# Second mixer of a two-layer network: 32x32 image products, norms applied on ScalarE, rows written out, VectorE's chains woven

## The reference, cut to what matters

```
u           = layernorm(x, 1e-6) @ W_in           # z (192), conv part (224 = 192 + 16 B + 16 C), dt (12)
xBC         = silu(conv3x3(conv part) + b_conv)
dt          = softplus(dt + dt_bias);  A = -exp(A_log)
L           = exp(segsum(dt * A))
Y_diag      = einsum('bclhn,bcshn,bhcls,bcshp->bclhp', C, B, L, X)
states      = einsum('bclhn,bhcl,bclhp->bchpn', B, decay_states, X)
Y_off       = einsum('bclhn,bchpn,bhcl->bclhp', C, states, exp(A_cumsum))
y           = layernorm(Y + D_param * X, 1e-5) * gamma + beta
x           = x + (y * silu(z)) @ W_out
```

## Time and profile before

| what | value |
| --- | --- |
| three runs, us | 2660.29, 2666.05, 2674.77 |
| profiled execution, own time | 2666.47 us |
| its span, first to last instruction | 2664.7 us |
| PE busy | 1986.0 us, 75% |
| DVE busy | 1728.5 us, 65% |
| POOL busy | 1371.1 us, 51% |
| ACT busy | 1063.6 us, 40% |
| mean granted TensorE clock | 0.805 |

### The profile page before, as it was taken

The page is one execution under the profiler, slowest core; times in us unless marked ns, Lnnn a source line. Parts: engine busy times, 40 slices in busy tenths (PEclk is TensorE's granted clock), DMA queues, the critical chain, the costliest instruction groups (busy, mean ns, idle before and its releaser), DMA issues.

```text
span 2664.7 us, 63187 instructions
## 1 busy us (share of the span) xinstructions
PE 1986.0 (75%) x24050; PEld 1660.2 (62%) x24050; DVE 1728.5 (65%) x5157; ACT 1063.6 (40%) x1936; POOL 1371.1 (51%) x1285
## 2 busy tenths in 40 slices
PE   3666433249999938999899989999975331699997
PEld 2555433237777727888788778888864331477775
DVE  4778644325766647888888878888856432366665
ACT  2233111037777723433333434333311110477775
POOL 2111155546877725555545545555533555477776
PEclk8667555569999968989998988899865555799999
DMA  7100011156666550000000000000000113466654
GB/s 140 39 21 21 6 50 51 65 207 208 203 208 207 166 95 2 3 3 3 3 3 2 3 3 3 2 3 2 3 2 18 52 53 124 138 210 206 205 194 126
DMA packets 99374, 203.29 MB, mean 76 GB/s; under 512 B 53158, under 2 KB 58911, under 8 KB 99096
## 3 DMA queue, kind: packets, MB, share of 16 engines
q10 hardware_dynamic: 21312, 102.00, 11.5%
q1 hardware_dynamic: 56024, 59.20, 8.3%
q0 software_dynamic: 21760, 38.33, 4.1%
HBM read 148.85 MB, written 52.58 MB: 76 GB/s over the span
## 4 chain that ended last, share of the span: by engine, by line
PE 26%; issue 14%; POOL 10%; DVE 8%; another core or an unknown queue 4%; DMA 1%; ACT 1%; SPq 0%; POOLq 0%; ACTq 0%; DVEq 0%
PE ps L938 4%; PE ps L939 4%; PE ps L940 4%; PE ps L1048 3%; POOL arena L663 3%; POOL w L644 2%; PE ps L1089 2%; PE ps L1109 2%; PE ps L970 2%; PE ps L1076 1%; POOL xn L655 1%; POOL arena L669 1%; PE ps L1093 1%; DVE arena L1159 1%
## 5 line engine op out<-in xcount | busy, mean ns | idle before, releaser
L1048 PE MATMUL ps<-rounded 128*128 128x224 f32 (+1 forms) x2256 | 373.3, 310 | 41.3 <-ACT rounded L801 18.2
L938 PE MATMUL ps<-rounded 97*128 97x512 f32 (+2 forms) x952 | 391.3, 411 | 9.2 <-issue 3.0
L1048 PEld LDWEIGHTS ps<-rounded 128*128 128x128 f32 x2256 | 325.7, 211 | 86.5 <-issue 33.9
L939 PE MATMUL ps<-rounded 97*128 97x512 f32 (+2 forms) x952 | 377.3, 396 | 0.0
L940 PE MATMUL ps<-rounded 97*128 97x512 f32 (+2 forms) x952 | 376.6, 396 | 0.0
L566 POOL DMA_INDIRECT rows<-arena x256 | 246.7, 964 | 216.2 <-DVEq L1453 140.6
L1520 DVE TENSOR_TENSOR rounded<-arena,rounded 128x512 fp32r<-128x512 f32 x296 | 225.4, 762 | 199.9 <-ACT arena L780 167.7
L779 ACT ACTIVATE rounded<-ps 128x512 fp32r<-128x512 f32 x444 | 267.5, 602 | 169.8 <-PE ps L940 138.5
L598 POOL TENSOR_TENSOR rounded<-arena,rounded 128x512 fp32r<-128x512 f32 x148 | 192.8, 1303 | 169.3 <-DVE arena L1503 94.1
L780 ACT ACTIVATE arena<-ps 128x512 f32<-128x512 f32 x444 | 267.1, 601 | 0.0
L970 PE MATMUL ps<-gw,arena 97*128 97x4 f32 x512 | 113.5, 347 | 172.6 <-issue 98.6
(11 more groups left out here) (229 smaller groups left out, 4358.5 us busy)
## 6 DMA issues: line engine op xcount, KB each, us to landing
rounded<-weights_by_expert ACTq DMA_DIRECT2D x148, 673.0 KB
arena<-rows SPq DMA_DIRECT2D x74, 392.0 KB
rows<-xn SPq DMA_DIRECT2D x17, 392.0 KB
residual<-in_x SPq DMA_DIRECT2D x16, 384.0 KB, 6.2
residual<-after_ffn SPq DMA_DIRECT2D x16, 384.0 KB, 6.0
weights_by_expert<-rounded SPq DMA_DIRECT2D x8, 672.0 KB, 3.2
rows<-arena POOLq DMA_INDIRECT x256
after_ffn<-arena POOLq DMA_INDIRECT x148
```

What stands on the lines that cost most here:

```text
L938: pe.matmul(dst, left[0], right[0], start=start, stop=False)
L939: pe.matmul(dst, left[1], right[0], start=False, stop=False)
L1048: pe.matmul(dst[:, 0:w], x3[:, x_part, n, slot, tokens], wtap[:, w_part, n, y + 1, 0:w], start=(y == 0 and n == x_part == w_part == 0), st ...
```

## The change

1. Tiles: L1073, L1085 and L1093 become four matmuls each, one for each image, on tiles of 32 partitions at most. `images_apart`, its three buffers and their clearing go; `bt` gets a second buffer.
2. Norms: VectorE no longer applies the norms. GpSimd adds a product (minus mean times the reciprocal deviation) behind its power, and ScalarE applies scale and bias, four activations of a norm, right behind its tanh of the same step: of y at r mod 4 = 2 (ahead of `shift_rest`), of x at r mod 4 = 3 (ahead of `affine`).
3. Rows: the hardware loop goes, all steps are written out with constant waits.
4. Weaving: the 14 operations of `time_steps`, and the moments of both norms, get chains (semaphores) of their own, and are put one by one between the operations of the row's other work.

```
+            def apply_norm(dst, src, own, has_rstd, count, done):
+                act.wait_ge(has_rstd, count)
+                for n in range(Q):
+                    ins = act.activation(dst(n), src(n), ACT.Identity, bias=own[:, 1, n:n + 1], scale=own[:, 5, n:n + 1])
+                ins.then_inc(done, 1)
             def step(g, r):                       # ScalarE
                 if (i := row(g, r, 0)) is not None:
                     conv_tanh(g, i)
+                if (c := quad(g, r, 10)) is not None:
+                    apply_norm(lambda n: u4[:, n, :], lambda n: yy[:, c % 2, n, :], moments_y, s["rstd_y"], c + 1, s["u"])
+                if (k := quad(g, r, -5)) is not None:
+                    apply_norm(lambda n: xn[:, k % 2 * Q + n, :], lambda n: rows_of[:, n, :], moments, rstd_ready, LN_MIX1 + k + 1, s["ln"])
                 if (k := quad(g, r, 1 - T_AHEAD)) is not None:
                     shift_rest(g, k)
...
+        def scale_and_bias(pool, ch, n, count, own):
+            pool.wait_ge(has_var, count)
+            ch.link(pool.tensor_tensor(mom[:, 5, 0:n], mom[:, 4, 0:n], half_neg[:, 0:n], ALU.pow))
+            pool.tensor_tensor(mom[:, 1, 0:n], mom[:, 0, 0:n], mom[:, 5, 0:n], ALU.mult).then_inc(has_rstd, 1)
...
-                pe.matmul(bank(4)[:, NH * SIDE:NH * SIDE + SIDE], b_apart[:, c % 2, i % Q, :], ct[:, c % 2, i % Q, :], start=True, stop=True)
+                for pb in images:
+                    of = slice(pb.start, pb.start + NS)
+                    pe.matmul(bank(4)[pb, NH * SIDE:NH * SIDE + SIDE], bt[of, c % 2, i % Q, :], ct[of, c % 2, i % Q, :], start=True, stop=True)
...
-                pe.matmul(bank(5)[:, INNER:2 * INNER], c_apart[:, c % 2, j, :], st[:, :, :].rearrange("p a b -> p (a b)"), start=True, stop=True)
+                for pb in images:
+                    of = slice(pb.start, pb.start + NS)
+                    pe.matmul(bank(5)[pb, INNER:2 * INNER], ct[of, c % 2, j, :], st[of, :, :].rearrange("p a b -> p (a b)"), start=True, stop=True)
...
-                pe.matmul(bank(6)[:, 0:INNER], b_rows[:, c % 2, j, :], xw[:, c % 2, j, :, :].rearrange("p a b -> p (a b)"), start=True, stop=True).then_inc(s["ds_pe"], 1)
+                for pb in images:
+                    ins = pe.matmul(bank(6)[pb, 0:INNER], xbc[pb, c % 2, j, INNER:CONV], xw[pb, c % 2, j, :, :].rearrange("p a b -> p (a b)"), start=True, stop=True)
+                ins.then_inc(s["ds_pe"], 1)
...
-            for r in range(-HEAD, TAIL):
+            for r in range(-HEAD, SIDE * G + TAIL):
                 if r == 0 and weights:
                     weights()
                 step(0, r)
-            with eng.Fori(0, G - 1) as g:
...
```

More of the change, by code:

```diff
@@ L65 @@
 HEAD, TAIL = 2 * Q, SIDE // 2
-CHAIN_MIX0, CHAIN_MIX1 = 52, 416
+CHAIN_MIX0 = 52
 def need(eng, sem, count):
@@ L1065, in sums @@
                 ins.then_inc(s["cs"], 1)
+            images = [slice(b * SIDE, (b + 1) * SIDE) for b in range(PACK)]
             def pairs(g, i):
@@ new lines, in norm_y, with norm_x @@
+            def norm_y(c, n):
+                if n:
+                    return moments_of(y_norm, INNER, 1e-5, n)
+                need(dve, s["u"], c)
+                ch.wait()
+                for row_ in range(Q):
+                    ch_norm.done(dve.bn_stats(stats_y[:, row_, :], yy[:, c % 2, row_, :]))
+            def norm_x(k, n):
+                if n:
+                    return moments_of(token_norm, D, 1e-6, n)
+                if k % NQ == 0:
+                    dve.wait_ge(x_in, 64 * (G + k // NQ + 1))
+                need(dve, s["ln"], k)
+                for row_ in range(Q):
+                    ch_norm.done(dve.bn_stats(stats[:, row_, :], quad_rows(0, k)[:, row_, :]))
@@ L1238, in step @@
             def step(g, r):
+                i, old, older = row(g, r, 0), row(g, r, 5), row(g, r, 6)
+                q, c12 = quad(g, r, 4), quad(g, r, 12)
+                cy, kx = quad(g, r, 9), quad(g, r, -6)
                 ch.wait()
-                if (c := quad(g, r, 12)) is not None:
-                    gate(g, c)
-                if (i := row(g, r, 0)) is not None:
+                if c12 is not None:
+                    gate(c12, 0)
+                if q is not None:
+                    time_steps(q, 0)
@@ L1248, in step @@
                 if (c := quad(g, r, 5)) is not None:
                     weigh(g, c)
-                if (q := quad(g, r, 4)) is not None:
+                if q is not None:
                     z_silu(g, q, 0)
-                if (i := row(g, r, 6)) is not None:
-                    gather(g, i)
-                if (i := row(g, r, 5)) is not None:
-                    attend(g, i)
+                    time_steps(q, 3)
+                if older is not None:
+                    gather_state(older)
@@ new lines, in step @@
+                if kx is not None:
+                    norm_x(kx, 3)
+                if older is not None:
+                    gather_skip(older)
+                if q is not None:
+                    time_steps(q, 7)
+                if kx is not None:
+                    norm_x(kx, 4)
+                if old is not None:
+                    attend_mask(old)
+                if q is not None:
+                    time_steps(q, 8)
+                if cy is not None:
+                    norm_y(cy, 0)
@@ L1256, in step @@
+                if old is not None:
+                    attend(old)
+                if q is not None:
+                    time_steps(q, 9)
+                if cy is not None:
+                    norm_y(cy, 1)
                 if (k := quad(g, r, -T_AHEAD)) is not None:
                     low(g, k)
-                if (q := quad(g, r, 5)) is not None:
-                    z_silu(g, q, 1)
-                if (q := quad(g, r, 4)) is not None:
-                    time_steps(g, q)
-                if (c := quad(g, r, 9)) is not None:
-                    norm_y(g, c, 0)
@@ L1264, in step @@
-                if (k := quad(g, r, -6)) is not None:
-                    norm_x(g, k, 0)
+                if cy is not None:
+                    norm_y(cy, 2)
+                if (c := quad(g, r, 5)) is not None:
+                    z_silu(g, c, 1)
+                if cy is not None:
+                    norm_y(cy, 3)
+                if q is not None:
+                    for n in range(10, 14):
+                        time_steps(q, n)
+                if cy is not None:
+                    norm_y(cy, 4)
```

210 lines of the change are left out of this document (130 added, 80 removed).

## The result

The changed kernel takes 2729.91 us (median of four runs, 2727.95 to 2730.88) against 2666.54 us before; the ratio is 1.0235 with a 95% interval of 1.0206 to 1.0263. It is slower by 63 us. The profiled execution took 2729.93 us, its span is 2728.1 us.

What follows compares the result with a forecast made beforehand. The prediction took the x3 loop as the bound: 18.2 + 1.2 + 5.7 + 7.1 = 32.2 us, plus 0.9 for clock, 33.1 a quad; +67 over 29 quads, less 8 for turns, gives 2725 us (range 2690 to 2765).

Steps and rivals of the forecast that it cites:

- The bound: Loop through several engines back to x3, which the convolution at r mod 4 = 3 awaits: 29.2 of 30.8 us a quad.
- The second loop: The scan waiting for L1159 gets the same delay as `low`, but was said to have room.
- D: ScalarE's `shift_most`, tanh and `shift_rest` up to x3: from 5.3 to 7.1 us (6.7 to 7.8) with four activations added.
- C: VectorE's `weigh`, gather, attend and `low` after the exp: from 5.0 to 5.7 us (4.0 to 5.9).
- B: `sums` and the exp of it: stays 1.2 us.
- A: TensorE's work from the convolution to `sums`: from 17.0 to 18.2 us (17.3 to 18.8), plus the 0.69 wait removed.
- The stall for the affine: TensorE's second u transposition waits for `affine`, queued behind ScalarE's norm of x: 0.8 us (0.3 to 1.1).
- The changes of form: TensorE switching between full and tiled products around `pairs`: 0.4 us in A (0 to 0.7).
- Clock: TensorE's low granted clock: 0.9 us a quad (0 to 3), where it had been 1.6.
- rival (3): More TensorE idling brings 1.2 GHz at the start of A: quad 35 us, 2780 us in all; chance 0.14.
- Rows written out: Removing the hardware loop's turns, seen at row 80: 8 us gained (0 to 12) for all turns.
- Tiles: Tiled products on TensorE cost what the full ones did, 0, apart from the changes of form.

Runs made afterwards that it cites:

- e2: The changed kernel with ScalarE applying the norm of y behind `shift_rest` instead of ahead of it: 2671.19 us, ratio 1.0027.
- e5: The changed kernel with ScalarE's four activations of the norm of y done twice at the same place: 2782.07 us, ratio 1.0439.
- e4: The kernel before with rows written out, image products as 32x32 tiles and `images_apart` gone; norms and VectorE's order as before: 2622.19 us, ratio 0.9834.
- e1: The changed kernel with VectorE applying both norms again, behind `conv_silu`: 2649.48 us, ratio 0.9937.
- e6: e1 with the statistics and first moments of y's norm behind `low` instead of ahead of `attend` and `low`: 2614.21 us, ratio 0.9796.
- e3: The kernel before with the rows written out and nothing else: 2642.40 us, ratio 0.9904.
- e11: The changed kernel with ScalarE's norm of y behind `shift_rest`, that of x behind `pair_decay`, and y's statistics behind `low`: 2615.36 us, ratio 0.9823.
- e12: e10 with GpSimd computing xd one step later, at r mod 4 = 2: 2622.95 us, ratio 0.9844.
- e10: e6 with `low` moved ahead of `attend_mask`: 2654.83 us, ratio 0.9964.
- e9: e6 with GpSimd computing xd early, at the start of the quad's first step: 2660.62 us, ratio 0.9991.

## Why the prediction was right

The forecast was 2725 us and 2730 was measured, and the largest term, the norms on ScalarE, acts by the loop that it named. Point by point:

- **The bound.** TensorE idles for x3 ahead of the convolution with r mod 4 = 3, up to 3.1 us. e2 (one move, -59 us) and e5 (a second dose, +52 us) show the mechanism apart from everything else.
- **The second loop.** Of the scan that waits for L1159 the prediction said that it "has room". The trace shows none: TensorE waited for that product in every quad before the change, 42.5 us in the window, four times what it waited for x3. The delay by `ny 0` went that way and not only through x3: against e4, e1 waits 9.5 us more for `attend` and 2.5 less for x3, and is 27 us slower.
- **D** was to be 7.1 us and is 7.1: four activations of 192 in 1.86 us, 0.47 each (bounds 0.36 to 0.55); GpSimd's power wasn't waited for. Those of 96 took 1.54 together, within 1.1 to 1.9.
- **C** was to be 5.7 and is 5.4: the statistics ahead of `attend` take 1.14 us and push its product onto xd, where it takes 1.30. e6 shows the statistics' place by itself, 35 us, but most of that is the wait for `attend`.
- **B** is 1.2.
- **A** was to be 18.2 and is 19.8, of which 2.2 is low clock; without it 17.6. The stall for the affine was to be 0.8 and is 0.48, and `sums` no longer waits. The changes of form that I charged with 0.4 don't show: with the tiles, scan and pairs became shorter by 0.2 us.
- **Clock.** I took 0.9 us a quad beyond the full-clock sum of 32.2. This quad had 2.2 beyond 31.4. That is what rival (3) described, 1.2 GHz at the start of A, where the convolution is on the loop, but at a smaller price than its quad of 35 us.
- **Rows written out** were credited with 8 us; e3 shows 24.
- **Tiles** were priced at 0 to +0.7 a quad (0.4 taken) and the end of `images_apart` at nothing for TensorE; e4 shows -0.7 for both together, 20 us in all.

The account of the medians: before 2666, rows -24, tiles -20, weaving with the statistics ahead +27 (e1 over e4), norms on ScalarE where they stood +80 (the changed kernel over e1): 2730. In the prediction the same four were -8, +12 (0.4 x 29), 0 (C's 0.7 against the 0.69 of `sums`) and +75 (1.8 and 0.8, x 29), with -20 for less low clock beside them. So mechanism and sign were right, and the norms' term nearly so, while the others were mis-sized and cancelled: rows and tiles gained 16 and 32 us more than I gave them; weaving cost 27 more, by the second loop, which the prediction had given room; and the 20 us of clock that I gave back did not come. That the sum came within 5 us is luck to that extent. Of what was to show it in the trace, everything is there: DVE below 700 us in the stage (601), quads of 33 us, row 80 like any other.

## What to carry to other kernels

When four engines run one software pipeline, moving work to an idle engine isn't free: what counts is what stands behind it in that engine's queue. Find the releaser of the wait that ends last, read that engine's order up to it, and put new work behind it; here the same eight activations cost 80 us or nothing by their place (the changed kernel over e1, e11 over e6). List the waits of a long window as well as of one quad: the second one can be as close behind as `attend` is here. When a change has several parts, take them apart even where the sum is as forecast: two of these four parts were gains of 24 and 20 us, hidden under a loss.

## What the runs showed of the hardware

- VectorE and GpSimd hold each other up, and whoever starts first goes through: attend's product (two SBUF operands) takes 0.56 us with GpSimd idle, 0.97 when it starts 0.4 us behind GpSimd's decay operand, and 1.83 when it starts 0.08 us behind xd; xd takes 1.81 us behind attend's product where it takes 1.49 else. Placing xd in another step moved the kernel by 32 and 46 us (e12 to e10, e6 to e9). The Trainium skill (GPSIMD Engine Reference, the row on SBUF interfaces) names the contention for two SBUF inputs, and the traces agree.
- Operations with one SBUF tensor as input differ. The four statistics aren't held up: 1.14 us beside xd, 1.13 with GpSimd idle (e12). TENSOR_SCALAR is: 1.48 us for 0.17 beside xd in e9, and 3.12 for 1.94 in e12. Operations that read PSUM kept their 0.35 us beside xw (L1183, L1188 and L1196 of the changed kernel's quad).
- In the changed kernel's window the granted clock is low behind 16 of the 17 waits for x3: after an idle time of 2.3 us the next 5.5 us had 0.52. The length of the idle time just ahead doesn't tell it: after 0.69 us (1371.10) the first six records of the convolution took 1.62 us, after 3.11 us (1405.11) they took 0.93 and the clock fell behind them, and in the kernel before they took 0.93 us after idle times of 1.1.
- A hardware loop of 32 rows and three turns cost 24 us against the same rows written out, less than half of it at the turn from row 79 to 80.
